# Linear attention with the bias added once and elu without relu, in a four-stage chain; gates applied at the second layer's experts; the last stage in halves

## The reference

```
x = layernorm(x + linear_attention(x))   # 16 heads of 8
x = layernorm(x + experts_top2(x))       # 8 experts, capacity 615 each
x = layernorm(x + causal_attention(x))   # 16 heads of 8, alibi
x = layernorm(x + experts_top4(x))       # 32 experts, and a shared one
out = x

def linear_attention(x):
    q, k, v = split(x @ w_qkv + b_qkv)
    q, k = elu(q) + 1, elu(k) + 1
    kv = einsum('bhnd,bhne->bhde', k, v)
    z = 1 / (einsum('bhnd,bhd->bhn', q, k.sum(2)) + 1e-8)
    return (einsum('bhnd,bhde->bhne', q, kv) * z) @ w_proj + b_proj

def experts_top4(x):
    s, idx = top_k(softmax(x @ router_w.T + router_bias), 4)
    s = s / s.sum(-1)
    h = silu(x @ gate_w[e].T) * (x @ up_w[e].T)     # for each expert e
    out = sum over k of s[k] * (h[idx[k]] @ down_w[idx[k]].T)
    return out + (silu(x @ sgate.T) * (x @ sup.T)) @ sdown.T
```

## Time and profile before

| | |
|---|---|
| median of three runs | 1549.73 us (1552.06, 1549.73, 1544.72) |
| the profiled execution's own time | 1547.14 us |
| its span, first to last instruction | 1545.2 us |
| mean granted TensorE clock | 0.825 of full speed |

### The profile page before, as it was taken

One profiled execution on the slowest core, in us unless ns is written; L12 is line 12 of the kernel. 1 busy time (PEld: TensorE's weight loads), 2 busy tenths in 40 slices (PEclk: granted clock), 3 DMA queues, 4 the chain that ended last, 5 costly groups with the idle time before them and its releaser, 6 DMA issues. The chain is left out here.

```text
span 1545.2 us, 20490 instructions
## 1 busy us (share of the span) xinstructions
PE 1080.8 (70%) x6847; PEld 645.3 (42%) x6848; DVE 809.3 (52%) x2132; ACT 503.4 (33%) x783; POOL 495.5 (32%) x500
## 2 busy tenths in 40 slices
PE   5761147752189999999899989886778677676500
PEld 3651135640124444544454444323454566666500
DVE  3767730001286887688877877831522232332347
ACT  1120013221106656665566545453211111111102
POOL 1110035643400310320154113243144255656622
PEclk9885558875559999999999989897899887888755
DMA  3223012216311222121222122015022322222043
GB/s 96 73 62 115 0 57 82 73 47 125 95 40 31 86 53 62 49 60 34 67 78 72 41 66 56 21 58 230 21 62 71 87 79 76 77 75 75 23 163 109
DMA packets 88789, 109.96 MB, mean 71 GB/s; under 512 B 16470, under 2 KB 68447, under 8 KB 85913
## 3 DMA queue, kind: packets, MB, share of 16 engines
q1 hardware_dynamic: 75362, 80.55, 18.1%
q0 software_dynamic: 13344, 28.33, 6.0%
HBM read 64.39 MB, written 42.04 MB: 69 GB/s over the span
## 5 line engine op out<-in xcount | busy, mean ns | idle before, releaser
L1853 DVE TENSOR_REDUCE maxima<-psum 128x1 f32<-128x512 f32 (+4 forms) x624 | 390.4, 644 | 126.1 <-PE psum L1675 68.7
L1789 ACT ACTIVATE probs<-psum 128x1024 f32<-128x1024 f32 (+3 forms) x384 | 300.7, 809 | 300.4 <-PE psum L1690 234.6
L1670 PE MATMUL psum<-ka,qa 75*128 75x512 bf16 (+3 forms) x768 | 243.7, 350 | 49.1 <-DMA ka<-in_c_alibi 28.8
L1686 PE MATMUL psum<-qa,ka 78*128 78x512 bf16 (+3 forms) x768 | 209.5, 335 | 6.4 <-DMA qa<-max_parts 3.2
L2300 POOL DMA_INDIRECT expert_out<-g_y,g_place x160 | 155.5, 972 | 128.2 <-DVE g_y L2271 77.2
L1703 PE MATMUL psum<-probs,v_wide 128*32 128x512 f32 (+3 forms) x1536 | 168.2, 511 | 0.2 <-ACT probs L1789 0.2
L1670 PEld LDWEIGHTS psum<-ka,qa 75*128 75x128 bf16 x768 | 69.3, 100 | 193.7 <-DVE maxima L1853 127.6
L1274 POOL DMA_INDIRECT sorted<-x_rows,to_row x64 | 62.6, 978 | 200.0 <-ACT probs L1789 128.9
L2271 DVE COPY g_y<-psum 128x512 f32<-128x512 f32 x40 | 27.7, 691 | 169.1 <-remote 125.0
L1686 PEld LDWEIGHTS psum<-qa,ka 78*128 78x128 bf16 x768 | 75.0, 101 | 79.3 <-ACT probs L1789 28.6
L2205 PE MATMUL psum<-w_down,g_hT 128*128 x320 | 57.7, 337 | 71.6 <-DVE g_hT L2265 71.6
(11 more groups left out here) (324 smaller groups left out, 1630.3 us busy)
## 6 DMA issues: line engine op xcount, KB each, us to landing
g_rows<-sorted SPq DMA_DIRECT2D x160, 64.5 KB
qa<-q_steps SPq DMA_DIRECT2D x48, 192.0 KB
ka<-k_steps SPq DMA_DIRECT2D x16, 576.0 KB
f_got<-expert_out SPq DMA_DIRECT2D x16, 512.0 KB, 5.9
expert_out<-blank POOLq DMA_DIRECT2D x1, 4096.0 KB, 16.9
w<-in_W SPq DMA_DIRECT2D x16, 256.0 KB
got<-expert_out SPq DMA_DIRECT2D x16, 256.0 KB, 3.7
w_gu<-in_gu SPq DMA_DIRECT2D x1, 4096.0 KB, 18.7
```

The source lines that it names most:

```text
L1670: mm = pe.matmul(bank[:, h * width:(h + 1) * width], qa[b][0:ROWS_MAX, h0 + h, qt * P:(qt + 1) * P], ka[b][0:ROWS_MAX, h0 + h, seg * HALF: ...
L1686: mm = pe.matmul(out, ka[s.buf][0:ROWS_ALL, h, j * P:(j + 1) * P], qa[s.buf][0:ROWS_ALL, h, q0:(c + 1) * HALF], start=True, stop=True, ski ...
L1789: act.activation(probs[k % PRING][:, 2 * pair:2 * pair + 2, 0:w], PS[:, 2 * pair:2 * pair + 2, 0:w], ACT.Exp).then_inc(exps, 1)
L1853: dve.tensor_reduce(maxima[:, seg, h0:h0 + heads, qt], bank[:, 0:heads * width].rearrange("p (h k) -> p h k", h=heads), AX.X, ALU.max).the ...
```

## The change

- **Linear attention.** elu(z)+1 is taken as max(min(exp(z), 1), z + 1), with the 1 added to q's and k's biases once, so `k_relu` is gone and k's exponential has a bias of -1. The projection's bias is added to all four batches of `x_rows` on POOL, ahead of the rounds, and `x_bias` is gone. The scaling of the rows goes from DVE to ACT, with a shift made on POOL. The loads count on two semaphores, `weights` (three: `w_qkv`, `bq`, `bkv`) and `more_weights` (five), for which PE and DVE wait behind the first front, and POOL ahead of its additions. `xT` is loaded first.
- **Route 0, experts 0.** POOL's clearing of the end of `sorted1` moves from the attention stage to route 0. The eleven weight loads of the attention stage move to the experts' stage, behind the loads of expert 1.
- **Head of attention.** The first six units go through four PSUM banks in turn. The alibi rows of steps 0 and 1 are loaded ahead of the second batch's results. DVE makes q's second remainder ahead of v's first half.
- **Gates.** DVE's `pick` makes the gates ahead of the rows. A scattered row has one column more, its gate, which POOL copies in with its place. In experts 1 DVE copies the gate of a group too (128x4), and the copy of y out of PSUM becomes a product with it.
- **Last stage.** Eight halves instead of four batches. All 16 loads are issued at once into four buffers. DVE adds the four expert rows to `acc` with four operations on 128x512; POOL makes power and shift on 128x4; ACT scales four tiles; SP stores a half.

```diff
+                sp.dma_start(xT[:], I["xT"][:, 0:SEQ]).then_inc(xT_here, 16)
                 sp.dma_start(w_qkv[:], I["w_qkv"]).then_inc(weights, 16)
-                sp.dma_start(xT[:], I["xT"][:, 0:SEQ]).then_inc(xT_here, 16)
                 sp.dma_start(bq[:], I["b_q_col"]).then_inc(weights, 16)
                 sp.dma_start(bkv[:], I["b_kv"].to_broadcast([P, KV])).then_inc(weights, 16)
-                sp.dma_start(head_mask[:], I["c_head_mask"]).then_inc(weights, 16)
-                sp.dma_start(w_proj[:], I["w_proj"]).then_inc(weights, 16)
-                sp.dma_start(bproj[:], I["b_proj"].to_broadcast([P, C])).then_inc(weights, 16)
-                sp.dma_start(w_r[:], I["Wr"]).then_inc(weights, 16)
-                sp.dma_start(b_r[:], I["br"].to_broadcast([P, E0])).then_inc(weights, 16)
+                sp.dma_start(head_mask[:], I["c_head_mask"]).then_inc(more_weights, 16)
...
-                pe.wait_ge(weights, 8 * 16)
+                pe.wait_ge(weights, 3 * 16)
...
-                act.wait_ge(weights, 8 * 16)
+                act.wait_ge(weights, 3 * 16)
+                act.wait_ge(biases_set, 3)
...
-                    act.activation(k_exp[:], kv[:, :, 0:C], ACT.Exp).then_inc(kexp_done, 1)
+                    act.activation(k_exp[:], kv[:, :, 0:C], ACT.Exp, bias=less_one[:]).then_inc(kexp_done, 1)
...
+                def scale(i):
+                    act.wait_ge(shift_ready, i + 1)
+                    wait_past(act, x_kept, i * 32)
+                    wait_past(act, xT_psum, i * 2)
+                    for t in range(TB):
+                        done = act.activation(x_new[:, t, :], y[:, t, :], ACT.Identity, bias=shift[:, t:t + 1],
+                                              scale=rstd[:, t:t + 1])
+                    done.then_inc(norm_done, 1)
...
-                pool.wait_ge(weights, 8 * 16)
+                pool.wait_ge(more_weights, 5 * 16)
                 pool.wait_ge(x_here, BATCH * 16)
+                for i in range(BATCH):
+                    pool.tensor_tensor(G.x_rows[:, tiles(i), :], G.x_rows[:, tiles(i), :],
+                                       bproj[:, None, :].to_broadcast([P, TB, C]), ALU.add).then_inc(xb_done, 1)
 
                 @repeat(pool, BATCH)
                 def _(i):
-                    wait_past(pool, y_taken, i * 2)
-                    pool.tensor_tensor(x_bias[:], G.x_rows[:, tiles(i), :],
-                                       bproj[:, None, :].to_broadcast([P, TB, C]), ALU.add).then_inc(xb_done, 1)
+                    wait_past(pool, norm_done, i)
                     emit_norm_pool(pool, G, NORMED + i, var_eps, rstd)
+                    pool.wait_ge(G.rstd_ready, NORMED + i + 1)
+                    pool.tensor_tensor(shift[:], less_mean[:], rstd[:], ALU.mult).then_inc(shift_ready, 1)
...
+                dve.memset(less_one[:], -1.0).then_inc(biases_set, 1)
+                dve.wait_ge(weights, 3 * 16)
+                dve.tensor_scalar(bq_more[:], bq[:], 1.0, None, ALU.add).then_inc(biases_set, 1)
+                dve.tensor_scalar(bkv[:, 0:C], bkv[:, 0:C], 1.0, None, ALU.add).then_inc(biases_set, 1)
+                dve.wait_ge(biases_set, 3)
...
-                    order.done(dve.tensor_scalar(k_relu[:], kv[:, :, 0:C], 0.0, None, ALU.max))
...
-                    dve.scalar_tensor_tensor(out=kv[:, :, 0:C], in0=k_exp[:], scalar=1.0, in1=k_relu[:],
-                                             op0=ALU.min, op1=ALU.add).then_inc(k_done, 1)
-                    assert order.count == 1
+                    dve.scalar_tensor_tensor(out=kv[:, :, 0:C], in0=k_exp[:], scalar=1.0, in1=kv[:, :, 0:C],
+                                             op0=ALU.min, op1=ALU.max).then_inc(k_done, 1)
...
+                    dve.tensor_scalar(less_mean[:], mv[:, :, 0], -1.0, None, ALU.mult)
+                    dve.tensor_scalar(var_eps[:], mv[:, :, 1], EPS, None, ALU.add).then_inc(G.var_ready, 1)
...
-                    emit_norm_scale(dve, G, NORMED + i, lambda t: y[:, t, :], mv, rstd,
-                                    lambda t: x_new[:, t, :]).then_inc(norm_done, 1)
...
+    def bank_of(self, unit):
+
+        n = SIDE_NO[unit]
+        return self.G.bank[n % FIRST_BANKS] if n < FIRST_UNITS else self.bank
...
+def emit_chain_weights(sp, S, I):
+
+    for dst, name in ((S.w_q, "Wq"), (S.w_k, "Wk"), (S.w_v, "Wv"), (S.b_q, "bq"), (S.b_k, "bk"),
+                      (S.w_o, "Wo"), (S.w_r, "Wr1")):
+        sp.dma_start(dst[:], I[name]).then_inc(S.weights, 16)
+    for dst, name in ((S.b_v, "bv"), (S.b_o, "bo"), (S.b_r, "br1")):
+        sp.dma_start(dst[:], I[name].to_broadcast(list(dst.shape))).then_inc(S.weights, 16)
+    sp.dma_start(S.goes_on[:].rearrange("p e t -> p (e t)"),
+                 I["c_goes_on1"].to_broadcast([P, E1 * TB])).then_inc(S.weights, 16)
...
+    if no >= FIRST_UNITS:
+        pe.wait_ge(S.side_read, no)
+    elif no >= FIRST_BANKS:
+        pe.wait_ge(S.side_read, no - FIRST_BANKS + 1)
...
+    pool.tensor_copy(source[:, :, PLACE_AT], G.place_of1[:, k, tiles(b)]).then_inc(S.placed, 1)
+    pool.tensor_copy(source[:, :, GATE_AT], G.gate1[:, tiles(b), k]).then_inc(S.placed, 1)
+    pool.wait_ge(S.placed, 2 * (b * K1 + k + 1))
...
+                for n in range(2):
+                    emit_load_alibi(sp, G, I, Step(n, n, 0))
...
-                for c in range(2):
-                    emit_side_vector(dve, S, Q, ("v", 0, c))
                 emit_rest(dve, S, Q, 0, 0)
+                emit_side_vector(dve, S, Q, ("v", 0, 0))
                 emit_last_part(dve, S, Q, 0, 0)
+                emit_side_vector(dve, S, Q, ("v", 0, 1))
...
+                    dve.wait_ge(gate_done, n + 1)
+                    dve.tensor_tensor(y[v][:], B[7].rearrange("p (s c) -> p s c", c=C),
+                                      gate[:, bass.ds(n * FT, FT), None].to_broadcast([P, FT, C]), ALU.mult).then_inc(y_done, 1)
...
+                    dve.tensor_copy(gate[:, bass.ds(n * FT, FT)], rows[v][:, :, GATE_AT]).then_inc(gate_done, 1)
...
+                for i in range(HALVES):
+                    pool.wait_ge(var_done, i + 1)
+                    pool.tensor_tensor(rstd[:, i], var_eps[:, i], G.minus_half[:, 0:HALF_TILES], ALU.pow).then_inc(rstd_done, 1)
+                    pool.wait_ge(rstd_done, i + 1)
+                    pool.tensor_tensor(shift[:, i], less_mean[:, i], rstd[:, i], ALU.mult).then_inc(shift_done, 1)
...
+                    dve.tensor_tensor(y, y, part[0], ALU.add).then_inc(summed, 1)
+                    dve.tensor_tensor(pair[:], part[1], part[2], ALU.add).then_inc(summed, 1)
+                    dve.wait_ge(summed, i * 4 + 1)
+                    dve.tensor_tensor(y, y, part[3], ALU.add).then_inc(summed, 1)
+                    dve.wait_ge(summed, i * 4 + 3)
+                    dve.tensor_tensor(y, y, pair[:], ALU.add).then_inc(summed, 1)
+                    dve.wait_ge(summed, i * 4 + 4)
+                    for j in range(HALF_TILES):
+                        last = dve.bn_stats(stats[:, j, :], y[:, j, :])
+                    order.done(last)
+                    for j in range(HALF_TILES):
+                        last = dve.bn_aggr(mv[:, j, :], stats[:, j, :])
+                    order.done(last)
+                    order.done(dve.tensor_scalar(less_mean[:, i], mv[:, :, 0], -1.0, None, ALU.mult))
+                    dve.tensor_scalar(var_eps[:, i], mv[:, :, 1], EPS, None, ALU.add).then_inc(var_done, 1)
...
+                rows = HALF * K1 // 2
+                for i in range(HALVES):
+                    for q in range(2):
+                        t = slice(rows_of(i).start + q * 2, rows_of(i).start + q * 2 + 2)
+                        sp.dma_start(got[i // 2][:, t].rearrange("p t k c -> p t (k c)"),
+                                     G.expert_out1[(2 * i + q) * rows:(2 * i + q + 1) * rows, :]
+                                     .rearrange("(t p k) c -> p t (k c)", p=P, k=K1)).then_inc(got_here[i], 16)
```

223 lines of the change are left out of this document (95 added, 128 removed).

## The result

The changed kernel takes 1503.87 us in the median of four executions (1499.15 to 1507.5), the kernel before 1550.52 us (four executions): a ratio of 0.9704, with a 95% interval of 0.9663 to 0.9745. The profiled execution has a span of 1505.8 us, 39.4 less than before, where the forecast had 37.5. The sum is close and its parts are not. The medians lie further apart, by 46.7 us: the profiled execution of the changed kernel was the slowest of its four, and the forecast went out from a profiled execution of before that was 2.6 us under its median. The measured 1503.87 us is 5.7 us under the forecast of 1509.6 and within its range.

What follows compares the result with a forecast made beforehand. No engine bounds the whole; TensorE has the attention steps, and other things pace the four places touched. Linear attention -10.4, head -9.6 and last stage -17.5 sum to -37.5, from 1547.1 to 1509.6 us, range 1499 to 1526.

Steps and rivals of the forecast that it cites:

- the forecast of -10.4: Linear attention: start -1.5, rounds -6.9 and -3.7, end +1.4, `less_mean` +0.3, together -10.4 us.
- the 3.0 that the prediction allows for it: Start of linear attention: gain if DVE never meets POOL, -2.4 from earlier weights and -0.6 from dropping `k_relu`.
- DVE can slip in: Start of linear attention: DVE gets in between two POOL additions, so it is slowed and not stopped; argued against +5.2.
- +5.2: Start of linear attention: cost in us if DVE waits for all four POOL additions, -2.4 + 4 x 1.9.
- The first rival: Start of linear attention: POOL's additions hold DVE up, +5.2 instead of -1.5, total 1516.5 us; chance 0.12.
- The bounds of -2 and -13: Linear attention: the least and most gain in us that the prediction allowed around its -10.4.
- The product: Head of attention: DVE's first product no longer waits for `goes_on` and ends 3.7 us earlier.
- PE's own two-microsecond products remain: Head, four banks: PE's products still pace the last four reads, saving about 0.9 us each, -3.6 in all.
- the term of 0: The 16 attention steps: operations left alone by the change, so no difference in time, 0 us.
- The second rival: Experts 1: the gates' copies delay POOL's scatters, 40 at 0.17 us, stage 6.8 us longer, total 1516.5; chance 0.10.
- The third rival: Last stage: the sixteen loads come mixed, first half late, at worst 15 us, total 1525 us; chance 0.08.
- The slower rival: Experts 1: y's product waits for the gate, so POOL waits in every group, +61 us, total 1571; chance 0.04.

Runs made afterwards that it cites:

- e2: The kernel before with only the linear attention part of the change: 1540.84 us, ratio 0.9944 to the kernel before.
- e7: The changed kernel with the first six units of the head of attention through one PSUM bank, as before the change: 1503.87 us (one execution).
- e8: The changed kernel with each of the six stores of q's and k's parts of batch 0 issued as four of 64 KB: 1495.09 us, ratio 0.9662.
- e6: The changed kernel with POOL's four additions held until `kv_heads` of round 0 is made: 1498.46 us, ratio 0.9663 to the kernel before.
- e12: The changed kernel with POOL's additions behind `kv_heads` of round 0 and batch 0's stores in four parts each: 1424.03 us on another chip, ratio 0.9638.
- e4: The kernel before with only the gates and last stage parts of the change: 1529.49 us, ratio 0.9867 to the kernel before.
- e9: The changed kernel with each group's gates copied five times instead of once in experts 1: 1430.23 us (one execution, another chip).
- e11: The changed kernel again, no edit, for a second trace: 1430.30 us (one execution, another chip, where the kernel before took 1476.1).
- e1: The kernel before again, no edit, for a second trace: 1553.35 us (one execution).
- e10: The changed kernel with the last stage's second-half loads issued only when the first half is there: 1433.69 us (one execution, another chip).
- e5: The kernel before with one edit, `pick` making the gates ahead of the rows: 1549.95 us (one execution).

## Why the prediction was right, and where it was not

**Linear attention: the places right, their sizes not.** The stage as a whole gives the forecast of -10.4 when DVE is first: -11.9 in e2, -10.3 in e7, -10.1 in e8, and -9.8 with the additions moved (e6). That agreement is luck in part, as the pieces show (us, against before, from the q products in the traces):

| piece | forecast | changed kernel | e7 |
|---|---|---|---|
| to the first q product | -1.5 | +0.3 | -4.4 |
| to the second | 0 | +2.1 | +0.1 |
| to the third | -6.9 | -5.2 | -6.7 |
| to the fourth | -3.7 | -2.0 | -2.3 |
| from there to route 0 | +1.7 | +1.6 | +3.0 |

The start without a meeting was worth 4.4 and not the 3.0 that the prediction allows for it: PE began 2.6 earlier, `k_relu` had taken 1.12 and not 0.6 on its path, and the k and v products took 3.82 us instead of 4.70, at a clock that rose earlier relative to them. With the meetings the start was 4.7 us later than in e7. The forecast had one meeting with POOL there, at 1.5; two came, and each cost 1.9 to 2.0. "DVE can slip in" between two additions was right, and so the +5.2 of a DVE that waits for all four did not come. The first rival, POOL's additions hold the start, was priced 6.7 us above the forecast, and the profiled execution came 7.0 above e7; but only 4.7 of these are the start, so that this agreement is luck too. The bounds of -2 and -13 for the stage do not follow from the prediction's own pieces: with -3.0 at the start these give -11.9, and with +5.2 and -5.8 they give +1.1. Which of the two starts first decides: a start 0.39 us behind the addition cost 2 us, and in e7, where DVE was 0.17 us ahead, its operation took 1.22. The Trainium skill, "SBUF — State Buffer", section "Who interferes with whom", has this as a lock held for a whole instruction; the traces agree, with 3.20, 2.15, 3.27 and 3.19 us behind an addition and 1.22 and 0.23 ahead of it or without one. The 2.15, like the 2.20 of the earlier trace rows, is a `kv_heads` with one tensor input in SBUF, so that two SBUF inputs are not needed for such a wait.

The other term that the forecast lacked is the clock. In the changed kernel's first trace it cost 2.7 us in the q product and the products behind it, and then it lengthened the second round, where PE's sums, behind the logits in its list and at a clock of 0.59 (3.47 us for the 1.95 of the round before), ended last; in the forecast DVE's list was the only bound. At full clock that round takes 19.1 us (e2, e6 to e12), near the forecast 18.9; the round behind it took 20.0 to 20.6 in every trace of the new list. That the meetings make the clock fall is not shown: in e4 and e12 nothing was blocked and the first q product ran at the low clock too, and in e9 to e11 PE was idle longest and it ran at the full one.

**Head: right in each step but the banks.** The product gave 3.7 (11.65 against 15.3 for the moments' start), as forecast. The stores' flow from the first store to SP's wait was 19.1 us, forecast 19.6. The failed step is "PE's own two-microsecond products remain", which put the banks at 3.6. From ACT's scaled rows to the first store it is 11.2 us with four banks and 17.9 in e7, 6.7 less, and 6.5 of it reach the end of the head. With free banks PE works ahead while ACT reads, so that at the clock of 0.50 two reads are 1.71 us apart instead of 2.86; and then the clock rises to 1.00, in all eight traces with four banks and in none of the six with one, and the last reads are 0.86 apart. Some 1.7 us of the 6.7 are the clock's.

**Steps: the term of 0 was wrong.** The work was the same, as forecast; its clock was not. Summing busy time times the missing share of the clock over all stretches of 2 us behind the first 60, I get about 15.7 us for the profile of before and 9.7 for the changed kernel's, 6.0 of the 7.4; over all runs it goes from 4.8 (e7, 625.4 us) to 16.5 (e1, 636.3 us). It is not chance from one trace to the next: the two traces of before took 636.3 and 636.3, the two of the changed kernel 628.9 and 628.7, on two chips, and e4, e9 and e10 took 628.5 to 629.3 with the drops at nearly the same places. The four traces with the old order of `pick` took 635.0 to 636.4, the ten with the new one 625.4 to 634.8. That the order moves it fits this but is not shown: e5, with the order alone, is one trace and took 633.7, and e6 and e12, which only have other additions in linear attention (and e12 other stores), took 634.8 and 634.5. Which pause of PE tips the clock was not found; between the pair of stretches shown above the wait of PE ahead of the drop is the same, 1.86 us. This stays open, and it is the size of the smaller terms of the sum.

**Last stage: right.** A half took 4.39 us for 4.34. DVE began 3.6 us earlier relative to the first load and not 2.7, and from its last operation to the end it was 5.9 us, not 6.7 (the terms that the prediction names for that tail add up to 6.4). With 0.3 more for the eight halves that is the difference, 1.4 us of 1.5.

**Gates in experts 1: right, at 0.** The second rival fell: five times the copies cost nothing (e9). The rule of the Trainium skill, "SBUF — State Buffer", section "SBUF: two separate sides", that a float32 copy within SBUF on DVE keeps GpSimd from writing the descriptors has no effect here that the stage's length shows: 160 further copies of 128x4, most of them beside a scatter, 0.0 to 0.4 us. Whether a copy of this shape is of the kind that the rule means, no run shows. The third rival, the last stage's loads mixed, fell with e10. The slower rival did not come: experts 1 stayed in the range of the kernel before. The tail's +1.6 is hardly more than the +1.2 of the kernel before from one trace to the next (e1).

So in the profiled execution the sum was right by errors against each other: linear attention gave 7.1 us less than forecast and the tail and the experts took 3.9, while the steps gave 7.4 more, the head 3.9 and the last stage 1.5.

## What to carry to other kernels

An operation on POOL that reads SBUF, started freely beside DVE's operations with two SBUF inputs, is a race and not a fixed cost: give it a semaphore that puts it beside DVE's work on PSUM, as e6 did. Where a share of the DMA engines stays at a quarter while nothing else runs, look at the outermost dimension of the transfer, and split it (e8). Take a gain on PE's path apart by the clock in its rows: part of the banks' gain was one. And where the clock moves, an edit in one stage can change the length of another whose instructions are the same (625.4 to 634.8 us for the steps of ten kernels' traces), and executions of one kernel lie 14 us apart: compare stage by stage, with more than one trace and many executions.

## What was not expected of the hardware

The changed kernel took 1430.3 us on one chip (one execution) and 1503.9 on another, and the kernel before 1476.1 against 1547.5 to 1550.5 on others. Between the changed kernel's two traces most of it lies in the two experts' stages (228.4 against 280.6 and 123.4 against 139.8 us), where POOL issues indirect transfers, and 6.2 us in the tail. In experts 1 the scatters of e11 follow each other with 0.30 us between them and wait for y 31.4 us in all, where the changed kernel's first profile has 86.6 us, and DVE's waits that the profile calls remote, whose releaser it does not find (126.7 us in front of `g_y`), are gone. The changed kernel's first trace and then e11:

```profile
L2321 DVE TENSOR_TENSOR g_y<-psum,g_gate 128x512 f32<-128x512 f32 x40 | 27.7, 692 | 167.5 <-remote 126.7 <-issue 25.2 <-PE psum L2254 15.6
```

```profile
L2321 DVE TENSOR_TENSOR g_y<-psum,g_gate 128x512 f32<-128x512 f32 x40 | 27.7, 692 | 105.3 <-issue 88.9 <-PE psum L2254 16.4
L2352 POOL DMA_INDIRECT expert_out<-g_y,g_place x160 | 155.5, 972 | 78.3 <-issue 46.9 <-DVE g_y L2321 31.4
```

A scatter takes the same 0.97 us on both. The granted clock of the stage differs too, 0.90 in e11 and 0.79 in the first trace, with PE busy for 157.0 and 186.8 us. Which of these comes first, and why one chip has them and the other not, no run shows. The ratio of the two kernels is about the same on both, 0.970 and 0.969 (the latter from one execution of the changed kernel).
